# Grouped attention of a four-layer kernel: the out-projection with the weights held, 512 tokens moving, fp32r products on split parts, and sums turned back once per batch

## Chip, cores and metric

The kernel runs on 1 core of one Trainium2 chip. The metric is the device time of one execution in microseconds (us). Three runs of the kernel before gave 2711.46, 2713.54 and 2714.96 us, with a median of 2713.54 us.

## What is computed

Four layers run one after the other on 4 batches of 512 tokens with 256 features, all in float32. The first is a windowed attention with 16 heads of 128, the second is the block this change lies in, the third is another attention, and the fourth is a mixture of experts. Around each layer stand a layer norm and a residual sum. The second layer begins with a grouped attention, which is all that the change touches:

```python
# 32 query heads, 8 key and value heads, head size 64; x is (4, 512, 256)
h = _rms(x, ln_w)
q = (h @ wq).reshape(B, S, NHEADS, HEAD_DIM)
k = (h @ wk).reshape(B, S, KVHEADS, HEAD_DIM)
v = (h @ wv).reshape(B, S, KVHEADS, HEAD_DIM)
q, k = _rope(q, k)
...
scores = jnp.einsum('bqhd,bkhd->bhqk', q, k) / np.float32(np.sqrt(HEAD_DIM))
scores = jnp.where(causal[None, None], scores, jnp.float32(-1e+30))
attn = jax.nn.softmax(scores, -1)
o = jnp.einsum('bhqk,bkhd->bqhd', attn, v).reshape(B, S, NHEADS * HEAD_DIM)
x = x + o @ wo
```

The out-projection is `o @ wo`: 2048 inputs to 256 outputs for each token.

## The kernel before

`attention1` (L896) works in **units**. A unit M is one batch and two query heads (one head of each key/value head of a pair), so there are 16 units for a batch and 64 in all. A unit has four **steps** S = 4M + j, and step j works on the token tile `tile_of(S)`: 0, 2, 1, 3 for j = 0 to 3. Tile t has t+1 blocks of 128 keys, so the rows it handles are 128, 384, 256 and 512 wide in the order of the steps. Every engine has its own queue, in an order written out by hand in one loop over the steps, and the queues meet at semaphores.

- **TensorE** (L1079 to L1095): in step S the scores of both heads (L1033, into one of four front banks `b_f` each); in j = 1 of some units a projection for later work (`beside`, L908: the keys of the next pair in units with m % 4 = 1, the values of the next batch in four units of a batch); in j = 1 the first half of the out-projection of unit M-3 (L1070); the transposes of step S-3 (L1043, one back bank `b_t` for each head); in j = 0 the queries of unit M+2 (L1020) and then the values product of unit M-2 (L1057, a back bank too); in j = 3 the second half of the out-projection of unit M-3.
- There are **two back banks**, taken in turn by everything that writes `b_t`. `back_free` (L998) makes TensorE wait until what was in the bank two uses ago has been read.
- **ScalarE** (L1132 to L1141): in step S first the copies of the transposed blocks of step S-3 out of the two back banks (`copy_pt`, L1105), then the exponentials of step S (L1114), then in j = 0 the copy of the values product to `ot` (`copy_out`, L1121), and in j = 1 the copy of a projected tile of values (`copy_v`, L1128).
- **VectorE** (L1186 to L1198): mask and row minimum of step S straight from the front banks (L1166), the reciprocals of step S-1 (L1174), the rotary products of each query and key projection (L1152, L1155), and once a batch the addition of the finished out-projection to the residual (`add_y`, L1180).
- **GpSimd** (L1226 to L1233): the normalising product of step S-1 (L1221) and the sums that end the rotary embedding (L1214).

The out-projection of a unit before has the tokens held and the weights moving. Each of four token tiles is a product of 128 inputs x 128 tokens with 128 x 256 weights:

```python
for t in (2 * half, 2 * half + 1):
    x = pe.matmul(p_y[half][:, t % 2 * DIM:(t % 2 + 1) * DIM], ot[:, M % 3, t * P:(t + 1) * P], wo[:, m, :],
                  start=(m == 0 and t % 2 == 0), stop=(m == B_UNITS - 1 and t % 2 == 1),
                  skip_group_check=True)
```

The banks `p_y` hold tokens in rows and sum over the 16 units of a batch. A float32 product stands in the trace as two matmul records (a transpose as one). Below, "the transposes of tile 3" are those of the step whose rows are 512 wide, 4 for each of two heads, and "the transposes of tile 0" are the two of the step with 128. In the first layer (`attention0`, not touched) the projections at L207 are already made in the manner that the change brings here: three fp32r products on a high and a low part of each operand; L342 and L565 there write such a high and such a low part.

Of the kernel before, what the change touches and what calls it, by code (L numbers as in the profile page):

```python
# [895 lines left out]
def attention1(nc, c, tables_in, wo_in):  # L896
# [19 lines left out]

    HEAD = [("v", 0, t) for t in range(TB)] + [("k", 0, 0), ("q", 0, 0), ("q", 1, 0)]
    fronts, backs = list(HEAD), []
    for S in range(LAST):
# [9 lines left out]
        if j == 0 and 0 <= M - 2 < UNITS:  # L929
            backs.append(("o", M - 2, 0))  # L930
    FRONT = {use: at for at, use in enumerate(fronts)}
# [4 lines left out]
    with ExitStack() as st:  # L936
# [15 lines left out]
        ot = sb("ot", [P, 3, SEQ])  # L952
# [7 lines left out]
        s_ov, s_ot, s_y, s_xn = sem("pv"), sem("ot_copied"), sem("out_proj"), sem("added")  # L960

# [15 lines left out]
        with nc.Block() as block:  # L977
# [7 lines left out]
            def _(pe):  # L985
# [12 lines left out]
                def back_free(use):  # L998
# [4 lines left out]
                    if kind == "t":  # L1003
                        pe.wait_ge(s_pt, 2 * i + n + 1)
                    else:
                        pe.wait_ge(s_ot, i + 1)
# [54 lines left out]
                def out_proj(M, half):  # L1061
                    m, b = M % B_UNITS, M // B_UNITS
                    if half == 0:
                        pe.wait_ge(s_ot, M + 1)
                        if m == 0 and b > 0:
                            pe.wait_ge(s_xn, b)
                        if M == 0:
                            pe.wait_ge(s_wo, 16)
                    for t in (2 * half, 2 * half + 1):
                        x = pe.matmul(p_y[half][:, t % 2 * DIM:(t % 2 + 1) * DIM], ot[:, M % 3, t * P:(t + 1) * P], wo[:, m, :],  # L1070
                                      start=(m == 0 and t % 2 == 0), stop=(m == B_UNITS - 1 and t % 2 == 1),
                                      skip_group_check=True)
                    if half == 1:
                        x.then_inc(s_y, 1)

# [3 lines left out]
                for S in range(LAST):  # L1079
# [12 lines left out]
                    if j == 0 and 0 <= M - 2 < UNITS:  # L1092
                        values(M - 2)
                    if j == 3 and ends:
                        out_proj(M - 3, 1)  # L1095

            @block.scalar
            def _(act):
# [18 lines left out]
                def copy_out(M):  # L1117
                    act.wait_ge(s_ov, M + 1)
                    if M >= 3:
                        act.wait_ge(s_y, M - 2)  # L1120
                    act.activation(ot[:, M % 3, :], back_bank(("o", M, 0))[:, :], ACT.Copy).then_inc(s_ot, 1)  # L1121
# [10 lines left out]
                for S in range(LAST):  # L1132
# [11 lines left out]
            def _(dve):  # L1144
# [1560 lines left out]
```

## Time and profile before

| | before |
|---|---|
| median of 3 runs | 2713.54 us |
| the profiled execution | 2709.55 us |
| its span | 2707.4 us |
| TensorE busy | 2346.0 us, 87% of the span |
| VectorE busy | 1624.5 us, 60% |
| ScalarE busy | 1299.8 us, 48% |
| GpSimd busy | 1294.4 us, 48% |
| TensorE records at L1070 (the out-projection changed here) | 512, 134.9 us busy |

The span is the time from the first to the last instruction of one profiled execution; that execution took 2709.55 us. Shares are means over four layers with different limits, so the stage of the change has to be read by itself. The grouped attention lasts from about 672 to 1502 us of the span. A record's own duration is longer than the time it keeps the engine from the next one, since matmuls and activations overlap with what follows; what an instruction costs its queue is the distance from its start to the next start.

### The profile page before, as it was taken

The numbers are of one execution on the slowest core, as the hardware profiler recorded it, in microseconds if no ns is written. First come the engines' busy times: TensorE is split into PE (matmuls) and PEld (weight loads), VectorE is DVE, ScalarE is ACT, GpSimd is POOL, SyncE is SP. The second block draws the span as 40 slices with busy tenths as digits, with TensorE's granted clock in tenths as the row PEclk, the third lists the DMA queues.
The fourth block names the chain that finished last, engine by engine and source line by source line (L and its number), as shares of the span: only waits on it lengthen the run. The fifth ranks groups of instructions, "written<-read, shape, count | busy, mean of one in ns | idle before, by whom it ended". The sixth has DMA issues, their size and how long they took to land. (4 is left out here: it accounts for less than half of the span.)

```text
span 2707.4 us, 41000 instructions
## 1 busy us (share of the span) xinstructions
PE 2346.0 (87%) x12100; PEld 1565.0 (58%) x12100; DVE 1624.5 (60%) x5263; ACT 1299.8 (48%) x3690; POOL 1294.4 (48%) x1301
## 2 busy tenths in 40 slices
PE   5999999996899999999999599992688887699992
PEld 5888888895455555555555456551334343566661
DVE  5767767666766766766776543335766753553334
ACT  3444444444555656656666344432265565343332
POOL 2444545441555555555555158870534310038883
PEclk8999999998999999999999689995799998699996
DMA  5000000011000000000000635553000000515555
GB/s 172 1 16 15 15 15 15 15 52 43 1 1 1 1 1 1 1 1 1 2 1 1 255 63 87 85 80 90 0 0 1 1 1 1 203 36 86 87 85 121
DMA packets 72817, 112.25 MB, mean 41 GB/s; under 512 B 11504, under 2 KB 59632, under 8 KB 72240
## 3 DMA queue, kind: packets, MB, share of 16 engines
q0 software_dynamic: 30336, 42.73, 10.1%
q1 hardware_dynamic: 42304, 67.34, 7.2%
q8 instruction: 88, 1.44, 0.2%
q14 instruction: 89, 0.73, 0.1%
HBM read 80.69 MB, written 36.32 MB: 43 GB/s over the span
## 5 line engine op out<-in xcount | busy, mean ns | idle before, releaser
L1221 POOL TENSOR_TENSOR b_sm<-b_sm,b_rden 128x128 f32<-128x128 f32 (+3 forms) x512 | 355.0, 720 | 355.5 <-DVE b_rden L1174 355.4
L1114 ACT ACTIVATE b_sm<-b_sm,b_mn 128x128 f32<-128x128 f32 (+3 forms) x512 | 284.8, 568 | 22.9 <-DVE b_mn L1166 21.6
L1105 ACT ACTIVATE b_pt<-b_t 128x128 f32<-128x128 f32 (+3 forms) x512 | 195.2, 438 | 143.1 <-PE b_t L1043 143.0
L1166 DVE CUSTOM_DVE_ANT_0 b_sm<-b_f,maskB 128x128 f32<-128x128 f32 (+3 forms) x512 | 233.5, 489 | 2.8 <-issue 1.7
L1033 PE MATMUL b_f<-b_k,b_q 64*128 64x128 f32 (+3 forms) x1024 | 209.6, 485 | 28.9 <-DVE b_prod L1155 14.5
L1155 DVE SCALAR_TENSOR_TENSOR b_prod<-b_f,b_sin 32x512 f32<-32x512 f32 x320 | 219.8, 687 | 4.3
L1590 POOL DMA_INDIRECT XN<-rows,m_slots x158 | 157.7, 998 | 94.0 <-issue 47.5
L2195 ACT ACTIVATE c_pt<-c_second 128x512 f32<-128x512 f32 x256 | 139.2, 598 | 123.6 <-PE c_second L2061 123.3
L2310 DVE TENSOR_REDUCE c_nm<-c_first 128x2 f32<-128x1024 f32 x128 | 155.1, 1220 | 69.8 <-PE c_first L2048 69.8
L1043 PE MATMUL b_t<-ident,b_sm 128*128 128x128 f32 x1280 | 193.2, 281 | 1.1 <-ACT b_pt L1105 0.8
L1043 PEld LDWEIGHTS b_t<-ident,b_sm 128*128 128x128 f32 x1280 | 142.2, 141 | 87.5 <-issue 60.3
L537 POOL TENSOR_TENSOR a_q<-a_prod 128x512 f32<-128x512 f32 x64 | 81.6, 1275 | 230.4 <-DVE a_prod L425 230.4
L1409 PE MATMUL m_p<-WM,Y 128*128 x316 | 153.8, 610 | 1.3 <-issue 1.3
L1057 PE MATMUL b_t<-b_pt,Y 128*64 128x512 f32 (+3 forms) x1024 | 152.0, 439 | 2.5 <-ACT b_pt L1105 2.5
L1020 PE MATMUL b_f<-HT,b_w 128*128 128x512 f32 x320 | 153.7, 604 | 0.0
L358 ACT ACTIVATE a_s<-a_s,a_nmx 128x192 f32<-128x192 f32 (+1 forms) x256 | 110.0, 431 | 89.0 <-DVE a_nmx L438 89.0
L1597 POOL DMA_INDIRECT acc<-Y,m_slots x79 | 125.3, 1587 | 32.6 <-issue 20.2
L1597 POOL DMA_INDIRECT acc<-m_plain,m_slots x79 | 125.4, 1587 | 30.1 <-issue 20.7
L1057 PEld LDWEIGHTS b_t<-b_pt,Y 128*64 128x64 f32 x1024 | 68.4, 136 | 117.1 <-issue 78.8
L1070 PE MATMUL b_y<-b_wo,b_ot 128*128 128x256 f32 x512 | 134.9, 387 | 0.0
L1033 PEld LDWEIGHTS b_f<-b_k,b_q 64*128 64x128 f32 x1024 | 78.7, 186 | 86.8 <-issue 62.2
L1787 DVE COPY Y<-m_p 128x256 f32<-128x256 f32 x79 | 33.5, 425 | 153.1 <-PE m_p L1419 133.7
(325 smaller groups left out, 5341.7 us busy)
## 6 DMA issues: line engine op xcount, KB each, us to landing
WM<-in_m_w_dram SPq DMA_DIRECT2D x4, 3072.0 KB, 17.2
WM<-in_m_w_dram SPq DMA_DIRECT2D x4, 2432.0 KB, 14.6
acc<-in_zeros_dram SPq DMA_DIRECT2D x3, 2176.0 KB, 15.2
n_part<-acc SPq DMA_DIRECT2D x12, 512.0 KB, 7.7
a_wa<-in_a_wa_dram SPq DMA_DIRECT2D x8, 512.0 KB, 4.3
b_w<-in_b_w_dram SPq DMA_DIRECT2D x1, 3072.0 KB, 10.3
XN<-rows,m_slots POOLq DMA_INDIRECT x158
X<-in_x_dram SPq DMA_DIRECT2D x4, 512.0 KB, 5.7
```

The source lines that it names most:

```text
L1033: pe.matmul(front_bank(("s", S, head))[:, 0:keys(t)], q_r[r, M % 3, t * P:(t + 1) * P], k_r[r, pg % 2, 0:keys(t)], start=True, stop=True). ...
L1043: x = pe.transpose(bank[:, k * P:(k + 1) * P], sm[:, slot(S, head), k * P:(k + 1) * P], c.ident[:, :])
L1057: x = pe.matmul(bank[r:r + B_HD, k * P:SEQ], v_s[:, b % 2, k, pair * P + r:pair * P + r + B_HD], pt[:, M % 2, head, k, k * P:SEQ], start=( ...
L1105: act.activation(pt[:, M % 2, head, 0:t + 1, t * P:(t + 1) * P], back_bank(("t", S, head))[:, 0:keys(t)].rearrange("p (k n) -> p k n", n=P ...
L1114: act.activation(sm[:, s, 0:keys(t)], sm[:, s, 0:keys(t)], ACT.Exp, scale=-1.0, bias=mn[:, s:s + 1], accum_out=den[:, s:s + 1]).then_inc(s ...
L1155: x = dve.scalar_tensor_tensor(to[dst, 1, :], bank[src, :], scale, sin[src, :], ALU.mult, ALU.mult)
L1166: dve.tensor_tensor_reduce(sm[:, s, 0:keys(t)], front_bank(("s", S, head))[:, 0:keys(t)], mask[:, SEQ - keys(t):SEQ], 1.0, -3 * NEG, ALU.a ...
L1221: pool.tensor_tensor(sm[:, s, 0:keys(t)], sm[:, s, 0:keys(t)], rden[:, s:s + 1].to_broadcast([P, keys(t)]), ALU.mult).then_inc(s_pn, 1)
L1409: x = pe.matmul(p_h[j % 2][:, 0:HC], lhs, rhs, start=(k == 0), stop=(k == 1))
L1590: pool.indirect_dma_start(out=xg[:, b % RING, :], out_offset=None, in_=rows_dram[:, :], in_offset=IOA(ap=slots[:, b:b + 1], axis=0)).then_ ...
L1597: pool.indirect_dma_start(out=acc_dram[b % 2][:, :], out_offset=IOA(ap=slots[:, b:b + 1], axis=0), in_=ys[:, b % 4, :], in_offset=None, co ...
L2310: dve.tensor_reduce(nm[:, t, 2 * j:2 * j + 2], two_banks(("max", f)), AX.X, ALU.max, negate=True).then_inc(s_nm, 1)
```

## The change

The out-projection of a unit holds the weights and lets the 512 tokens of the batch move: for each half of the 256 outputs three fp32r products (high weights by high sums, high by low, low by high). The banks `p_y` then hold outputs in rows and tokens in columns. For this `ot` and the unit's weights are each split: ScalarE copies the high parts (`ot_hi`, `wo_hi`, both fp32r) and GpSimd subtracts to get the low ones (`ot_lo`, `wo_lo`). Once per batch VectorE copies the two banks to `y_t`, TensorE transposes them back in two halves of four transposes, each into a back bank, and VectorE adds each to the residual.

```diff
+    def turned_back(S):
+        M, j = S // STEPS_OF, S % STEPS_OF
+        if j == 2 and M >= B_UNITS and M % B_UNITS in (4, 5):
+            return ("z", M // B_UNITS - 1, M % B_UNITS - 4)
+        return None
...
+        if turned_back(S) is not None:
+            backs.append(turned_back(S))
+    backs += [("z", BATCH - 1, half) for half in range(2)]
...
                     if kind == "t":
                         pe.wait_ge(s_pt, 2 * i + n + 1)
+                    elif kind == "z":
+                        pe.wait_ge(s_xn, 2 * i + n + 1)
...
                 def out_proj(M, half):
                     m, b = M % B_UNITS, M // B_UNITS
                     if half == 0:
-                        pe.wait_ge(s_ot, M + 1)
+                        pe.wait_ge(s_ol, M + 1)
                         if m == 0 and b > 0:
-                            pe.wait_ge(s_xn, b)
-                        if M == 0:
-                            pe.wait_ge(s_wo, 16)
-                    for t in (2 * half, 2 * half + 1):
-                        x = pe.matmul(p_y[half][:, t % 2 * DIM:(t % 2 + 1) * DIM], ot[:, M % 3, t * P:(t + 1) * P], wo[:, m, :],
-                                      start=(m == 0 and t % 2 == 0), stop=(m == B_UNITS - 1 and t % 2 == 1),
+                            pe.wait_ge(s_yc, b)
+                        pe.wait_ge(s_wl, M + 1)
+                    cols = slice(half * P, (half + 1) * P)
+                    w_hi, w_lo = wo_hi[:, M % 3, cols], wo_lo[:, M % 3, cols]
+                    o_hi, o_lo = ot_hi[:, M % 2, :], ot_lo[:, M % 2, :]
+                    for n, (weight, o) in enumerate(((w_hi, o_hi), (w_hi, o_lo), (w_lo, o_hi))):
+                        x = pe.matmul(p_y[half][:, :], weight, o, start=(m == 0 and n == 0), stop=(m == B_UNITS - 1 and n == 2),
                                       skip_group_check=True)
...
+                def turn_back(use):
+                    _, b, half = use
+                    pe.wait_ge(s_yc, b + 1)
+                    back_free(use)
+                    for t in range(2):
+                        for k in range(KD):
+                            at = (2 * half + t) * P
+                            x = pe.transpose(back_bank(use)[:, t * DIM + k * P:t * DIM + (k + 1) * P], y_t[:, k, at:at + P],
+                                             c.ident[:, :])
+                    x.then_inc(s_z, 1)
...
+                    if turned_back(S) is not None:
+                        turn_back(turned_back(S))
                     if j == 3 and ends:
                         out_proj(M - 3, 1)
+                for half in range(2):
+                    turn_back(("z", BATCH - 1, half))
...
+                def high_out(M):
+                    act.wait_ge(s_ot, M + 1)
+                    if M >= 2:
+                        act.wait_ge(s_y, M - 1)
+                    act.activation(ot_hi[:, M % 2, :], ot[:, M % 2, :], ACT.Copy).then_inc(s_oh, 1)
+
+                def high_weights(M):
...
+                    act.activation(wo_hi[:, M % 3, :], wo[:, M % B_UNITS, :], ACT.Copy).then_inc(s_wh, 1)
...
+                    if j == 1 and 0 <= M - 2 < UNITS:
+                        high_out(M - 2)
+                        high_weights(M - 2)
...
-                def add_y(b):
+                def copy_y(b):
                     dve.wait_ge(s_y, (b + 1) * B_UNITS)
-                    for a in range(2):
-                        to = c.XN[:, b * TB + 2 * a:b * TB + 2 * a + 2, :].rearrange("p t d -> p (t d)")
-                        x = dve.tensor_tensor(to, p_y[a][:, :], to, ALU.add)
-                    x.then_inc(s_xn, 1)
+                    if b > 0:
+                        dve.wait_ge(s_z, 2 * b)
+                    for k in range(2):
+                        x = dve.tensor_copy(y_t[:, k, :], p_y[k][:, :])
+                    x.then_inc(s_yc, 1)
+
+                def add_y(use):
+                    _, b, half = use
+                    dve.wait_ge(s_z, 2 * b + half + 1)
+                    to = c.XN[:, b * TB + 2 * half:b * TB + 2 * half + 2, :].rearrange("p t d -> p (t d)")
+                    dve.tensor_tensor(to, back_bank(use)[:, :], to, ALU.add).then_inc(s_xn, 1)
...
+                    if S >= 1 and turned_back(S - 1) is not None:
+                        add_y(turned_back(S - 1))
...
+                def low_weights(M):
+                    pool.wait_ge(s_wh, M + 1)
...
+                    pool.tensor_tensor(wo_lo[:, M % 3, :], wo[:, M % B_UNITS, :], wo_hi[:, M % 3, :].bitcast(F32),
+                                       ALU.subtract).then_inc(s_wl, 1)
+
+                def low_out(M):
+                    pool.wait_ge(s_oh, M + 1)
...
+                    pool.tensor_tensor(ot_lo[:, M % 2, :], ot[:, M % 2, :], ot_hi[:, M % 2, :].bitcast(F32),
+                                       ALU.subtract).then_inc(s_ol, 1)
...
+                    if j == 3 and 0 <= M - 2 < UNITS:
+                        low_weights(M - 2)
+                        low_out(M - 2)
+                for M in range(UNITS - 2, UNITS):
+                    low_weights(M)
+                    low_out(M)
```

`copy_out` now also waits for the low part of the unit before the last, and `ot` has two buffers where it had three.

How the queues change is shown at three places. The first is ScalarE's queue over one unit, from the copies of tile 1 (128x2x128) to the copy to `ot`. Before:

```order
L1105 ACTIVATE b_pt<-b_t 128x2x128 x2
L1114 ACTIVATE b_sm,b_den<-b_sm,b_mn 128x384 x2
L1105 ACTIVATE b_pt<-b_t 128x4x128 x2
L1114 ACTIVATE b_sm,b_den<-b_sm,b_mn 128x256 x2
L1105 ACTIVATE b_pt<-b_t 128x128 x2
```

And with the change (L1137 are the copies of L1105, L1146 the exponentials of L1114):

```order
L1137 ACTIVATE b_pt<-b_t 128x2x128 x2
L1146 ACTIVATE b_sm,b_den<-b_sm,b_mn 128x384 x2
L1159 ACTIVATE b_ot_hi<-b_ot 128x512
L1166 ACTIVATE b_wo_hi<-b_wo 128x256
L1137 ACTIVATE b_pt<-b_t 128x4x128 x2
L1146 ACTIVATE b_sm,b_den<-b_sm,b_mn 128x256 x2
L1137 ACTIVATE b_pt<-b_t 128x128 x2
```

Two copies stand between the exponentials and the copies of tile 3, and so ahead of the copies that free the back banks for tile 0.

The second place is TensorE's queue in the unit after the one in which VectorE copied the sums of a batch, with the transposes that turn them back (L1100; L1059 are the transposes of L1043, L1049 the scores, L1088 the out-projection):

```order
L1088 MATMUL b_y<-b_ot_hi,b_wo_lo 128x512
L1059 MATMUL b_t<-ident,b_sm 128x128 x4
L1049 MATMUL b_f<-b_k,b_q 128x256 x2
L1059 MATMUL b_t<-ident,b_sm 128x128 x8
L1100 MATMUL b_t<-ident,b_y_t 128x128 x4
L1049 MATMUL b_f<-b_k,b_q 128x512 x2
L1059 MATMUL b_t<-ident,b_sm 128x128 x2
```

Before, the same stretch of TensorE's queue read:

```order
L1043 MATMUL b_t<-ident,b_sm 128x128 x4
L1033 MATMUL b_f<-b_k,b_q 128x256 x2
L1043 MATMUL b_t<-ident,b_sm 128x128 x8
L1033 MATMUL b_f<-b_k,b_q 128x512 x2
L1043 MATMUL b_t<-ident,b_sm 128x128 x2
```

Four transposes with a bank of their own stand between those of tile 3 and those of tile 0. The third place is VectorE's queue at the same point (L1214 is the mask and minimum, L1222 the reciprocals, L1236 the addition to the residual):

```order
L1213 MEMSET tick 128x1
L1214 ISA b_sm,b_mn<-b_f,maskB 128x512
L1214 ISA b_mn 128x1
L1222 RECIPROCAL b_rden<-b_den 128x1 x2
L1236 TENSOR_TENSOR XN<-b_t,XN 128x512
L1213 MEMSET tick 128x1
L1214 ISA b_sm,b_mn<-b_f,maskB 128x128
```

The addition that empties that bank comes after the minima and reciprocals of the step that TensorE issues after the turning back.

## Rows read from the trace of the kernel before

**Rows 1.** Busy time by stretch: PE, PEld, DVE, ACT, POOL, then PEclk, DMA share, GB/s

```profile
1000.00:1400.00 400.00, 390.39 (x2082) 214.56 (x2082) 284.26 (x1212) 246.31 (x796) 222.09 (x291) 1.00 0.00 1
```

**Rows 2.** Waits between 1000 and 1400 us: total us, times, longest

```profile
ACT b_pt L1105 <- PE b_t L1043: 71.1, 31, 3.2
DVE tick L1165 <- PE b_f L1033: 58.1, 86, 2.3
```

**Rows 3.** Timeline of TensorE, a plain unit: start us, us, engine, line, operation

```profile
1134.80 1.13 PE L1070 MATMUL b_y<-b_wo,b_ot 128*128 128x256 f32 x4
1135.77 0.60 PE L1043 MATMUL b_t<-ident,b_sm 128*128 128x128 f32 x4
...
1136.93 1.09 PE L1043 MATMUL b_t<-ident,b_sm 128*128 128x128 f32 x8
1137.95 1.13 PE L1033 MATMUL b_f<-b_k,b_q 64*128 64x512 f32 x4
1139.01 0.44 PE L1043 MATMUL b_t<-ident,b_sm 128*128 128x128 f32 x2
1139.29 1.03 PE L1070 MATMUL b_y<-b_wo,b_ot 128*128 128x256 f32 x4
1140.24 0.49 PE L1033 MATMUL b_f<-b_k,b_q 64*128 64x128 f32 x4
...
1146.34 1.13 PE L1070 MATMUL b_y<-b_wo,b_ot 128*128 128x256 f32 x4
```

**Rows 4.** Timeline of ScalarE in the same unit

```profile
1136.18 0.66 ACT L1105 ACTIVATE b_pt<-b_t 128x256 f32<-128x256 f32 x2 [1.52 <-PE b_t L1043]
1136.73 0.62 ACT L1114 ACTIVATE b_sm<-b_sm,b_mn 128x384 f32<-128x384 f32 x1
...
1137.92 1.08 ACT L1105 ACTIVATE b_pt<-b_t 128x512 f32<-128x512 f32 x2
1138.88 0.52 ACT L1114 ACTIVATE b_sm<-b_sm,b_mn 128x256 f32<-128x256 f32 x1
```

**Rows 5.** Groups of instructions in the first layer: busy us, mean ns

```profile
L565 POOL TENSOR_TENSOR a_wb_parts<-a_wb,a_wb_parts 128x512 fp32r<-128x512 f32 x8 | 10.2, 1271 | 52.3 <-ACT a_wb_parts L342 52.3
...
L342 ACT ACTIVATE a_wb_parts<-a_wb 128x512 fp32r<-128x512 f32 x8 | 4.9, 617 | 0.0
```

**Rows 6.** Timeline of TensorE in the first layer, fp32r products with 512 moving

```profile
403.77 1.55 PE L207 MATMUL p_q<-HT_part,a_wa_parts 128*128 128x512 f32 x6
405.16 1.53 PE L207 MATMUL p_k<-HT_part,a_wa_parts 128*128 128x512 f32 x6
406.52 3.62 PE L274 MATMUL p_s<-a_wo,a_ot 128*128 128x256 f32 x16
```

**Rows 7.** Timeline of a unit with a key projection beside it

```profile
959.12 1.13 PE L1033 MATMUL b_f<-b_k,b_q 64*128 64x512 f32 x4 [0.72 <-DVE b_prod L1155]
960.17 0.44 PE L1043 MATMUL b_t<-ident,b_sm 128*128 128x128 f32 x2
...
958.30 1.07 ACT L1105 ACTIVATE b_pt<-b_t 128x512 f32<-128x512 f32 x2
```

**Rows 8.** Timeline of a unit with a values projection beside it

```profile
972.35 0.59 ACT L1128 ACTIVATE Y<-b_f 128x512 f32<-128x512 f32 x1
...
972.83 1.08 ACT L1105 ACTIVATE b_pt<-b_t 128x512 f32<-128x512 f32 x2
973.08 1.13 PE L1033 MATMUL b_f<-b_k,b_q 64*128 64x512 f32 x4 [0.64 <-ACT Y L1128]
```

**Rows 9.** Timeline of VectorE in the plain unit of rows 3

```profile
1139.25 0.69 DVE L1166 CUSTOM_DVE_ANT_0 b_sm<-b_f,maskB 128x512 f32<-128x512 f32 x1
...
1140.49 0.22 DVE L1174 RECIPROCAL b_rden<-b_den 128x1 f32<-128x1 f32 x2
```

**Rows 10.** Timeline of GpSimd in the same unit

```profile
1140.73 3.18 POOL L1221 TENSOR_TENSOR b_sm<-b_sm,b_rden 128x256 f32<-128x256 f32 x4 [0.58 <-DVE b_rden L1174]
```

**Rows 11.** Timeline of the stage's end

```profile
1496.67 3.72 PE L1070 MATMUL b_y<-b_wo,b_ot 128*128 128x256 f32 x16
...
1496.79 0.60 ACT L1121 ACTIVATE b_ot<-b_t 128x512 f32<-128x512 f32 x1 [2.53 <-PE b_t L1057]
...
1500.43 1.29 DVE L1180 TENSOR_TENSOR XN<-b_y,XN 128x512 f32<-128x512 f32 x2 [12.47 <-PE b_y L1070]
```

More of the change, by code:

```diff
@@ L951, in attention1 @@
         pt = sb("pt", [P, 2, 2, TB, SEQ])
-        ot = sb("ot", [P, 3, SEQ])
+        ot, ot_hi, ot_lo = sb("ot", [P, 2, SEQ]), sb("ot_hi", [P, 2, SEQ], F32R), sb("ot_lo", [P, 2, SEQ], F32R)
+        wo_hi, wo_lo = sb("wo_hi", [P, 3, DIM], F32R), sb("wo_lo", [P, 3, DIM], F32R)
+        y_t = sb("y_t", [P, 2, SEQ])
         front, back = [pb(f"f{i}") for i in range(4)], [pb(f"t{i}") for i in range(2)]
@@ L960, in attention1 @@
         s_ov, s_ot, s_y, s_xn = sem("pv"), sem("ot_copied"), sem("out_proj"), sem("added")
+        s_oh, s_ol, s_wh, s_wl = sem("ot_high"), sem("ot_low"), sem("wo_high"), sem("wo_low")
+        s_yc, s_z = sem("y_copied"), sem("y_turned_back")
         def tile_of(S):
@@ L1118, in copy_out @@
                     act.wait_ge(s_ov, M + 1)
+                    if M >= 2:
+                        act.wait_ge(s_ol, M - 1)
+                    act.activation(ot[:, M % 2, :], back_bank(("o", M, 0))[:, :], ACT.Copy).then_inc(s_ot, 1)
+                def high_out(M):
+                    act.wait_ge(s_ot, M + 1)
+                    if M >= 2:
+                        act.wait_ge(s_y, M - 1)
+                    act.activation(ot_hi[:, M % 2, :], ot[:, M % 2, :], ACT.Copy).then_inc(s_oh, 1)
+                def high_weights(M):
+                    if M == 0:
+                        act.wait_ge(s_wo, 16)
                     if M >= 3:
                         act.wait_ge(s_y, M - 2)
-                    act.activation(ot[:, M % 3, :], back_bank(("o", M, 0))[:, :], ACT.Copy).then_inc(s_ot, 1)
+                    act.activation(wo_hi[:, M % 3, :], wo[:, M % B_UNITS, :], ACT.Copy).then_inc(s_wh, 1)
                 def copy_v(job):
@@ L1192, in _ @@
                     if j == 0 and M > 3 and M % B_UNITS == 3:
-                        add_y(M // B_UNITS - 1)
+                        copy_y(M // B_UNITS - 1)
+                    if S >= 1 and turned_back(S - 1) is not None:
+                        add_y(turned_back(S - 1))
                     if j == 0 and M + 2 < UNITS:
@@ L1197, in _ @@
                         rotate(beside(M))
-                add_y(BATCH - 1)
+                copy_y(BATCH - 1)
+                for half in range(2):
+                    add_y(("z", BATCH - 1, half))
             @block.gpsimd
@@ L1222, in normalise @@
                                            ALU.mult).then_inc(s_pn, 1)
+                def low_weights(M):
+                    pool.wait_ge(s_wh, M + 1)
+                    if M >= 3:
+                        pool.wait_ge(s_y, M - 2)
+                    pool.tensor_tensor(wo_lo[:, M % 3, :], wo[:, M % B_UNITS, :], wo_hi[:, M % 3, :].bitcast(F32),
+                                       ALU.subtract).then_inc(s_wl, 1)
+                def low_out(M):
+                    pool.wait_ge(s_oh, M + 1)
+                    if M >= 2:
+                        pool.wait_ge(s_y, M - 1)
+                    pool.tensor_tensor(ot_lo[:, M % 2, :], ot[:, M % 2, :], ot_hi[:, M % 2, :].bitcast(F32),
+                                       ALU.subtract).then_inc(s_ol, 1)
                 for job in HEAD[TB:]:
```

## The prediction

> **What bounds the kernel now.** I read the busy time by stretch first. In the middle of the grouped attention TensorE is busy 390 of 400 us at its full granted clock (1.00, the 2.4 GHz level); VectorE is at 284, ScalarE at 246, GpSimd at 222 [rows 1]. That says TensorE's work sets the stage. The waits agree: ScalarE waits for transposes and VectorE for scores [rows 2]. A saving on TensorE would then count in full, and work added to ScalarE or GpSimd would be free. The mean hides who is *just* in time, so the timelines of one unit come next. A plain unit runs from 1134.80 to 1146.34 us, 11.54 us [rows 3]. ScalarE idles before the copies of tile 1, then runs without a gap: copies of tile 1 at 1136.18, exponentials of 384 at 1136.73, copies of tile 3 from 1137.92 to 1139.00 [rows 4]. TensorE needs the back bank of the second of these for the second transpose of tile 0. The two transposes start at 1139.01 and the next product at 1139.29 [rows 3], so one takes about 0.13 us and the second starts at 1139.14. A bank or buffer that ScalarE frees reaches TensorE about 0.11 to 0.14 us after its copy's end (972.35 + 0.59 = 972.94, scores at 973.08 [rows 8]); I take 0.11. So the second transpose could not have begun before 1139.11. **This link has 0.03 us to spare**, and that is exactly where the change puts two copies.
>
> **The change part by part.**
>
> *Out-projection on TensorE.* Before, a half costs 1135.77 − 1134.80 = 0.97 and 1140.24 − 1139.29 = 0.95 us [rows 3]. Sixteen such records in a row at the end take about 3.72 − 0.38 = 3.34 us to the last start, 0.22 each [rows 11], so 4 are 0.86 to 0.89 and some 0.1 is the first weight load after narrower work. An fp32r product with 512 moving costs (405.16 − 403.77)/6 = 0.232 and (406.52 − 405.16)/6 = 0.227 us [rows 6]; three are 0.69, with the same first load 0.80. So **0.16 to 0.17 us less for a half, 0.34 for a unit**. Without the first load it would be 0.5 for a unit. That is small because a float32 product of 256 already costs only about twice an fp32r product of 512.
>
> The Trainium skill (TensorE: Matmul & The Clock Gate, Back-to-back issue gap) gives about 131 ns as the sustained spacing at 512 moving columns. By that the saving would be about 0.9 us a unit; the rows here say 0.23 us for the same count, in a stream with weight loads, and the sum goes by them.
>
> *Two copies on ScalarE, each unit.* Copies of 512 cost (1138.88 − 1137.92)/2 = 0.48 us start to start, of 256 (1136.73 − 1136.18)/2 = 0.275 [rows 4]. A copy from SBUF to fp32r lasts 617 ns [rows 5] where `copy_out` from PSUM lasts 0.60 [rows 11]; so 0.02 more. Together **0.78 us**. They lie between the exponentials of 384 and the copies of tile 3. These then end at 1139.00 + 0.78 = 1139.78, and TensorE's second transpose starts at 1139.89 instead of 1139.14: a stall of 0.75 us. The half saved ahead of it moves both queues alike. A plain unit comes to 0.75 − 0.34 = +0.41 us. Behind the stalled transpose stand the other half of the out-projection, the scores of the next unit and the queries' projection, so nothing passes it. Bounds of the two copies: 0.62 (a fifth off) and 617 + 400 ns of whole duration, 1.0.
>
> The Trainium skill (ScalarE: Activation LUTs, Rules for kernel authors) budgets about 0.3 us for each ACTIVATE plus 0.83 ns an element: 0.73 + 0.51 = 1.24 us for the pair, an estimate from that page. It would put about 20 us on the sum. The trace shows the next copy starting 0.48 us after one of 512, so I stay with the rows.
>
> *Units with a values projection.* Here TensorE already waits 0.64 us for `copy_v` [rows 8], which stands behind the new copies in ScalarE's queue: +0.78 − 0.34 = +0.44 us.
>
> *Units with a key projection.* Here the scores of 512 wait 0.72 us for VectorE's rotary products, and the copies of tile 3 end at 959.37, so the transpose at 960.17 + 0.13 has 0.8 us to spare [rows 7]. The new copies fit. The first half's saving is lost in VectorE's wait, the second's stays: −0.17 us.
>
> *GpSimd.* Low weights and low sums are subtractions of 256 and 512 columns; 512 cost 1271 ns [rows 5]; half the columns cost at least half, I take 0.73; 2.0 us in all. They follow the normalising of tile 1, which starts at 1140.73 and takes some 1.2 of the 3.18 us (two of the four products, the narrower ones) [rows 10]; with ScalarE's 0.78 of delay that ends at 1142.7, the low parts at 1144.7. The out-projection needs them at 1146.3, and GpSimd has 178 of 400 us idle [rows 1]. Cost zero while those 1.6 us hold; if they went, every excess would stall the first half directly.
>
> *Turning back.* Twice per batch, for three batches inside the loop. In a plain unit, the turned back half needs the bank of tile 3's first head, copied at 1137.92 + 0.78 + 0.60 = 1139.30; TensorE starts at 1139.41 instead of going on at 1137.95. Four transposes take 0.51 us (8 take 1.02 [rows 3]), so the scores of 512 start at 1139.92. VectorE starts its minimum 1.30 us after the scores, which started at 1137.95, and ends its reciprocals at 1140.71, 1.46 later [rows 9]; then comes the addition of about 0.65 to 0.69 (two in 1.29 [rows 11]). The bank is free at 1139.92 + 1.30 + 1.46 + 0.69 + 0.11 = 1143.48, and the second transpose of tile 0 waits for it: 4.34 us later than 1139.14, and no second stall for ScalarE. Net +4.0 us. The other half falls in a unit with a key projection; the same sum from 958.30 gives a start at 963.69 instead of 960.30, net +3.2 us. The two copies of VectorE take the place and about the time of the two old additions.
>
> *End.* Before: values, copy to `ot` until 1497.39, last product, additions from 1500.43 to 1501.72 [rows 11]. TensorE had the out-projection of the unit before last as cover. Now the last unit's copy is followed by the high copies (about 1.0 with the hand-over), the low weights (0.73) and low sums (1.27), then six products (1.4), their drain, two copies (1.3), eight transposes with an addition behind each half (about 2): the end falls near 1505.7, **+4 us**.
>
> *Sum.* The copies run for units 2 to 63: 14 with a key and 12 with a values projection, 3 plain and 3 key units with a turned back half, 33 other plain ones. 33 × 0.41 + 12 × 0.44 − 11 × 0.17 + 3 × 4.0 + 3 × 3.2 + 4 = 13.5 + 5.3 − 1.9 + 12 + 9.6 + 4 = **+42.5 us**. Against the profiled execution's 2709.55 us that is 2752 us. The median of the runs shown lies 4 us above that execution, 2756 from there; I say 2753. A measurement of this kernel can tell 0.2%, about 5 us, from no change.
>
> **The rivals.**
> A. *TensorE alone sets the stage* (ends faster). Place: the banks at tile 0's transposes. If ScalarE's two copies cost its queue less than about 0.34 us a unit, or TensorE has unseen slack there, no stall comes and the turned back halves cost only their 0.51 us: −62 × 0.34 + 3 + 4 = −14 us, 2696. For: 97% busy, and ScalarE 38% idle [rows 1]. Against: 0.03 us of slack by the rows, and no copy of 256 or 512 that costs so little. 7%.
> B. *The copies hide, the turned back halves don't*: −21 + 18 + 4, about 2711, no change. 6%.
> C. *The products come at the faster spacing.* If an fp32r product of 512 cost 0.13 us, as one of 256 might, each half would save 0.3 more: 48 units with two halves that count and 14 with one are −33 us, 2720. The skill's spacing named above would do this. Against: rows 6. 5%.
> D. *Dearer copies.* At 1.0 to 1.24 us a pair the 45 units that stall add 10 to 20 us: 2763 to 2773. The ScalarE page's rule is this one. 10%.
> E. *GpSimd is late.* If the subtractions cost over 3.6 us a unit (1.6 more than the rows), or are held back behind VectorE, the first half waits; a further 0.5 us on each of 62 units gives 2784. 4%.
> That the products split into more passes (the change not doing what it says) would need fp32r at 512 to act otherwise than in rows 6; it lies in what is left with E.
>
> **How the numbers follow.** The forecast has 66%, its own range 2740 to 2762 from the bounds of the copies (45 units × 0.16 to 0.22) and a turned back half a quarter cheaper. With A 7, B 6, C 5, D 10, E 4 and 2 for the rest, the range 2718 to 2774 leaves out A, B and E. Faster: A, some of B: 9%. Within 0.2%: most of B: 5%. Slower: 86%.
>
> **What the changed profile would show.** Right: the grouped attention lasts about 873 us instead of 830; TensorE's share in its middle falls toward 91%; waits of TensorE for the copies of tile 3 of about 0.75 us in plain units, which were absent; the scores after a values projection wait 1.4 us; six waits of about 2 us for the addition to the residual; an out-projection half of about 0.8 us; no waits for GpSimd's low parts. Wrong: plain units of 11.2 us with no wait at tile 0 (A); waits on the subtractions (E); three products in about 0.4 us (C).

## The result, and the profile after

Four runs of the changed kernel gave 2760.72 to 2773.98 us with a median of **2766.59 us**; the kernel before gave 2714.05 us (median of 4). The ratio is 1.0199, with a 95% interval of 1.0184 to 1.0215: slower, by 52.5 us, where 2753 was forecast in a range of 2718 to 2774. The number lies inside that range, but above the forecast's own 2740 to 2762.

| | before | after |
|---|---|---|
| median | 2714.05 us | 2766.59 us |
| profiled execution (span) | 2709.55 (2707.4) us | 2773.98 (2772.2) us |
| first scores of the stage to its last residual addition | 683.5 to 1501.7: 818.2 us | 682.9 to 1554.3: 871.4 us |
| plain unit | 11.54 us | 12.03 us |
| unit with a key projection | 14.05 us | 13.87 us |

The profiled execution after was the slowest of its four, and 11.6 us of its longer span lie outside the stage: most of them in the third layer, not touched, where it was granted a lower clock in places (0.93 against 0.98 in the stretch of its middle). So the stage's own length, **+53.2 us**, is what the readings below go by, and it is close to the difference of the medians (52.5).

The busy time by stretch, in the columns of [rows 1]:

```profile
1000.00:1400.00 400.00, 365.57 (x1900) 193.72 (x1900) 266.48 (x1140) 256.55 (x812) 267.93 (x335) 0.99 0.00 1
```

TensorE fell from 390 to 366 us busy in 400. It has not handed the bound to an engine that is full: the next, GpSimd, stands at 268. TensorE now waits. The whole execution's waits of TensorE for its own operands, in the order of the trace's answer on the lines of the scores and of the transposes:

```profile
  ACT Y L1173: 17.5, 12
  DVE b_prod L1203: 16.0, 14
...
  ACT b_pt L1137: 20.3, 68
```

`b_pt` are the copies out of the back banks: 68 waits where there were 2. `Y` is the copy of projected values: 12 waits, each 1.46 us where it was 0.64. The same answer names GpSimd's normalising product (`b_sm`) for another 54.8 us ahead of these transposes (13.6 before); that GpSimd isn't what they wait for is shown below by e4 and e6. Now a plain unit on TensorE, the rows that answer to [rows 3]:

```profile
1142.58 0.50 PE L1088 MATMUL b_y<-b_ot_hi,b_wo_hi 128*128 128x512 f32 x1
1142.92 0.39 PE L1088 MATMUL b_y<-b_ot_lo,b_wo_hi 128*128 128x512 f32 x1
1143.15 0.39 PE L1088 MATMUL b_y<-b_ot_hi,b_wo_lo 128*128 128x512 f32 x1
1143.38 0.60 PE L1059 MATMUL b_t<-ident,b_sm 128*128 128x128 f32 x4
...
1145.56 1.13 PE L1049 MATMUL b_f<-b_k,b_q 64*128 64x512 f32 x4
1147.10 0.30 PE L1059 MATMUL b_t<-ident,b_sm 128*128 128x128 f32 x1 [0.40 <-ACT b_pt L1137]
1147.58 0.30 PE L1059 MATMUL b_t<-ident,b_sm 128*128 128x128 f32 x1 [0.19 <-ACT b_pt L1137]
1147.64 0.48 PE L1088 MATMUL b_y<-b_ot_hi,b_wo_hi 128*128 128x512 f32 x1
...
1148.51 0.49 PE L1049 MATMUL b_f<-b_k,b_q 64*128 64x128 f32 x4
```

And ScalarE's queue at the same time, against [rows 4]:

```profile
1145.54 0.62 ACT L1159 ACTIVATE b_ot_hi<-b_ot 128x512 fp32r<-128x512 f32 x1
1146.06 0.41 ACT L1166 ACTIVATE b_wo_hi<-b_wo 128x256 fp32r<-128x256 f32 x1
1146.36 1.07 ACT L1137 ACTIVATE b_pt<-b_t 128x512 f32<-128x512 f32 x2
```

The first half of the out-projection takes 1143.38 − 1142.58 = 0.80 us. The two copies take 1146.36 − 1145.54 = 0.82 us of ScalarE's queue. The copies of tile 3 end at 1147.43, and the second transpose of tile 0 starts at 1147.58, 0.15 us behind them, instead of the 1146.75 that TensorE's own queue ahead of it (1145.56 + 1.06 + 0.13) would allow: a stall of 0.83 us. The half behind it starts 0.06 us after that transpose (0.15 before) and takes 1148.51 − 1147.64 = 0.87 us (0.95 before): 0.17 us saved from the transpose on, as much as in the first half.

A unit with a turned back half, against the working in the prediction:

```profile
953.05 0.63 PE L1100 MATMUL b_t<-ident,b_y_t 128*128 128x128 f32 x4 [1.46 <-ACT b_pt L1137]
...
956.28 0.68 DVE L1236 TENSOR_TENSOR XN<-b_t,XN 128x512 f32<-128x512 f32 x1
...
957.10 0.30 PE L1059 MATMUL b_t<-ident,b_sm 128*128 128x128 f32 x1 [2.10 <-POOL b_sm L1280]
957.16 0.51 PE L1088 MATMUL b_y<-b_ot_hi,b_wo_hi 128*128 128x512 f32 x1
957.48 0.62 PE L1088 MATMUL b_y<-b_ot_lo,b_wo_hi 128*128 128x512 f32 x1
957.89 0.63 PE L1088 MATMUL b_y<-b_ot_hi,b_wo_lo 128*128 128x512 f32 x1
```

The first wait is the 1.46 us that the prediction's rows give (1137.95 to 1139.41). The second is named after GpSimd's normalising, but that transpose waits for two things, and the other one came last: VectorE's addition that empties the bank (`add_y`), which starts at 956.28 and takes 0.68 us, so it ends 0.14 us before the transpose. In e1 below, three of the six waits of 2.10 us are named after this addition. A releaser's name in such a row is a hint, the queue's own order decides. The unit took 15.59 us from second transpose to second transpose (941.51 to 957.10), the one with the key projection after it 18.84 (to 975.94).

The records after 957.4 show something else: 0.62 us where such a product is 0.39. The granted clock of the stretches behind the wait:

```profile
941.00:957.00 16.00, 12.33 (x67) 6.63 (x67) 9.99 (x45) 10.08 (x33) 10.12 (x15) 1.00 0.00 1
957.00:962.00 5.00, 4.90 (x18) 3.25 (x18) 0.70 (x8) 3.41 (x11) 4.39 (x5) 0.66 0.02 3
962.00:967.00 5.00, 5.00 (x25) 2.04 (x24) 4.24 (x10) 0.62 (x2) 0.14 (x1) 1.00 0.00 0
```

For some of the 5 us after the two waits TensorE ran at the lower level (1.2 GHz). The Trainium skill (TensorE: Matmul & The Clock Gate, HAM oscillation) says that waits between stretches of TensorE's work can bring its clock down. The trace agrees in part: with the same waits of 1.46 and 2.10 us ahead, the clock fell behind the first turned back half of each of the three batches (0.66, 0.72 and 0.76 over the next 5 to 7 us) and stayed at the full level behind the second half of each (1.00 over the next 5 us).

The same happens at two other places, and it matters for the comparisons below. In the second unit of the stage TensorE waits 1.18 and 2.29 us in every kernel here. The kernel before goes on at the full clock, the changed one doesn't, and its unit takes 1.27 us more. The stretch from 708 to 712 us, before and after:

```profile
708.00:712.00 4.00, 3.80 (x18) 1.77 (x16) 2.33 (x20) 3.87 (x15) 3.82 (x5) 1.00 0.01 2
708.00:712.00 4.00, 4.00 (x13) 2.39 (x14) 1.90 (x15) 3.41 (x13) 4.00 (x6) 0.57 0.01 2
```

In this unit e3 and e4 of the experiments below ran at the lower level too, and e1, e2 and e5 to e9 at the full one. The other place is the last unit's six products, behind a wait of 2.09 us: 0.43 us apart in the kernel after, 0.23 in e1, e2 and e3. Each of the two is worth 1.2 to 1.9 us of stage. No edit explains them: e1 and e3 run the same instructions in the second unit, and e3 and e7 in the last products, and still differ there.

### The profile page after: what moved, and what is told of

Same layout as the page of the kernel before. It is cut to its first block and busy times, and to the rows that moved or that the text cites. A ratio compares the mean times of both kernels' runs of the same rounds, so it can differ in the third digit from the quotient of the medians.

```text
span 2772.2 us, 41329 instructions
## 1 busy us (share of the span) xinstructions
PE 2356.4 (85%) x12004; PEld 1555.1 (56%) x12004; DVE 1632.3 (59%) x5271; ACT 1350.7 (49%) x3818; POOL 1418.1 (51%) x1429
## 5 line engine op out<-in xcount | busy, mean ns | idle before, releaser
L1146 ACT ACTIVATE b_sm<-b_sm,b_mn 128x128 f32<-128x128 f32 (+3 forms) x512 | 284.9, 569 | 19.0 <-DVE b_mn L1214 18.9
L1137 ACT ACTIVATE b_pt<-b_t 128x128 f32<-128x128 f32 (+3 forms) x512 | 196.2, 438 | 151.6 <-PE b_t L1059 151.0
L1049 PE MATMUL b_f<-b_k,b_q 64*128 64x128 f32 (+3 forms) x1024 | 210.0, 487 | 38.5 <-ACT Y L1173 17.5
L1214 DVE CUSTOM_DVE_ANT_0 b_sm<-b_f,maskB 128x128 f32<-128x128 f32 (+3 forms) x512 | 233.7, 489 | 3.7 <-issue 2.5
L1059 PE MATMUL b_t<-ident,b_sm 128*128 128x128 f32 x1280 | 201.9, 284 | 33.2 <-ACT b_pt L1137 20.3
L1059 PEld LDWEIGHTS b_t<-ident,b_sm 128*128 128x128 f32 x1280 | 145.4, 142 | 129.5 <-issue 71.7
L1049 PEld LDWEIGHTS b_f<-b_k,b_q 64*128 64x128 f32 x1024 | 79.1, 187 | 98.4 <-issue 79.1
L1213 DVE MEMSET tick<- 128x1 f32 x512 | 30.2, 59 | 160.1 <-PE b_f L1049 154.0
```

Source lines behind the costliest of these rows:

```text
L1049: pe.matmul(front_bank(("s", S, head))[:, 0:keys(t)], q_r[r, M % 3, t * P:(t + 1) * P], k_r[r, pg % 2, 0:keys(t)], start=True, stop=True). ...
L1059: x = pe.transpose(bank[:, k * P:(k + 1) * P], sm[:, slot(S, head), k * P:(k + 1) * P], c.ident[:, :])
L1137: act.activation(pt[:, M % 2, head, 0:t + 1, t * P:(t + 1) * P], back_bank(("t", S, head))[:, 0:keys(t)].rearrange("p (k n) -> p k n", n=P ...
L1146: act.activation(sm[:, s, 0:keys(t)], sm[:, s, 0:keys(t)], ACT.Exp, scale=-1.0, bias=mn[:, s:s + 1], accum_out=den[:, s:s + 1]).then_inc(s ...
L1214: dve.tensor_tensor_reduce(sm[:, s, 0:keys(t)], front_bank(("s", S, head))[:, 0:keys(t)], mask[:, SEQ - keys(t):SEQ], 1.0, -3 * NEG, ALU.a ...
```

## The experiments

The runs e1 to e4, e5 to e8 and e9 each have the kernel before measured beside them on the same chip. Stage lengths are from the first scores to the last residual addition, one profiled execution each; the kernel before has 818.2 us. Units of a kind that no edit touches take the same time within 0.03 us in all of them, except where the clock fell at the two places named above; where a comparison crosses these, their share is given. So the stage settles terms that the whole kernel's time, which scatters by some us for reasons in other layers, can't.

| run | whole, median us | before in that group | ratio, 95% interval | stage us |
|---|---|---|---|---|
| e1_high_early | 2721.78 | 2710.85 | 1.0048 (1.0032 to 1.0065) | 830.5 |
| e2_turn_early | 2738.47 | 2710.85 | 1.0108 (1.0091 to 1.0126) | 846.9 |
| e3_both_moves | 2700.13 | 2710.85 | 0.9964 (0.9952 to 0.9975) | 809.1 |
| e4_before_copies | 2751.37 | 2710.85 | 1.0150 (1.0133 to 1.0167) | 859.1 |
| e5_float32_held | 2714.64 | 2709.78 | 1.0013 (1.0003 to 1.0022) | 823.2 |
| e6_low_twice | 2702.39 | 2709.78 | 0.9968 (0.9955 to 0.9981) | 811.1 |
| e7_values_first | 2698.73 | 2709.78 | 0.9950 (0.9933 to 0.9967) | 801.3 |
| e8_one_product | 2667.77 | 2709.78 | 0.9839 (0.9822 to 0.9855) | 777.0 |
| e9_end_shorter | 2694.69 | 2714.17 | 0.9931 (0.9917 to 0.9944) | 798.4 |

**The place of the copies in ScalarE's queue.** The changed kernel, with:

```diff
                         copy_out(M - 2)
-                    if j == 1 and 0 <= M - 2 < UNITS:
                         high_out(M - 2)
                         high_weights(M - 2)
```

> ScalarE's two high copies are issued in step j = 0 right behind the copy to ot, where ScalarE has been idle, and no longer between the exponentials of 384 and the copies of tile 3. Theory (the copies' place in ScalarE's queue stalls TensorE at the transposes of tile 0): the waits there go, a plain unit takes about 11.25 us instead of 12.03, the wait behind a values projection falls from 1.46 to about 0.68 us, the waits before the turned back halves too; 51 times 0.78 = 40 us less than the changed kernel, about 2727 us. Rival (the split work loads GpSimd or memory, wherever it stands): no change, about 2766 us.

```profile
1137.15 1.13 PE L1049 MATMUL b_f<-b_k,b_q 64*128 64x512 f32 x4
1138.21 0.44 PE L1059 MATMUL b_t<-ident,b_sm 128*128 128x128 f32 x2
```

The stage fell from 871.4 to 830.5, by 40.9 us; 2.5 of them are the clock, which fell in the second unit and in the last products after, and did not here. The waits of TensorE for `b_pt` at tile 0 are down from 68 to the 2 that were there before the change, those behind a values projection are back at 0.64, and the wait before a turned back half is 0.64 where it was 1.46; the 2.10 us behind it stayed. A plain unit takes 11.21 us. The same two copies, the same subtractions and products, some 38 us apart by their place alone.

The reverse, the kernel before with only the copies added, in the place that the change gives them:

```diff
+                def high_copies(M):
+                    act.wait_ge(s_ot, M + 1)
+                    act.activation(ot_hi[:, M % 2, :], ot[:, M % 3, :], ACT.Copy)
...
+                    act.activation(wo_hi[:, M % 3, :], wo[:, M % B_UNITS, :], ACT.Copy)
...
+                    if j == 1 and 0 <= M - 2 < UNITS:
+                        high_copies(M - 2)
```

> The kernel before, with nothing but the two high copies added to ScalarE's queue where the change has them (nobody reads what they write). Theory: 36 plain units stall 0.75 us and 12 with a values projection 0.78 us, units with a key projection not at all: 36 us more than the kernel before, about 2750 us. Rival (TensorE alone sets the stage, ScalarE has 38% idle): no change, 2714 us.

The stage went to 859.1 us, +40.9, of which 1.2 are the clock in the second unit, and the whole kernel to 1.0150 of its time. The rows of two units:

```profile
1148.06 0.30 PE L1044 MATMUL b_t<-ident,b_sm 128*128 128x128 f32 x1 [0.40 <-POOL b_sm L1231]
1148.54 0.30 PE L1044 MATMUL b_t<-ident,b_sm 128*128 128x128 f32 x1 [0.19 <-ACT b_pt L1106]
1160.42 0.30 PE L1044 MATMUL b_t<-ident,b_sm 128*128 128x128 f32 x1 [0.40 <-POOL b_sm L1231]
```

A plain unit takes 12.36 us (1148.06 to 1160.42) where it took 11.54: 0.82, the whole of the copies' time, and so does a unit with a values projection; 48 × 0.82 = 39.4 us. Nothing was added to GpSimd here, and the first transpose still bears its name: the product that it reads (128x128) had ended at 1145.93, and ScalarE's first copy of tile 3 ended at 1147.93, 0.13 us ahead of it. Copies that nobody reads cost some 40 us on an engine that idles a third of the stage.

**The place of the turned back halves.** The changed kernel, with:

```diff
-        if j == 2 and M >= B_UNITS and M % B_UNITS in (4, 5):
+        if j == 0 and M >= B_UNITS and M % B_UNITS in (4, 5):
...
-                    if S >= 1 and turned_back(S - 1) is not None:
-                        add_y(turned_back(S - 1))
                     if j == 0 and M + 2 < UNITS:
                         rotate(("q", M + 2, 0))
+                    if turned_back(S) is not None:
+                        add_y(turned_back(S))
```

> Only the turned back halves move: TensorE issues them in step j = 0 behind the values product, VectorE adds them behind the rotary products of the same step. Theory (a half costs because of the banks that it waits for and holds, not for its four transposes): a unit with a turned back half falls from 15.6 to about 12.6 us (plain) and from 18.8 to about 14.5 us (key); 22 us less than the changed kernel, about 2744 us, and TensorE's granted clock stays at 1.00 in these units. Rival (the transposes and additions themselves are the price): at most 3 us less.

```profile
940.42 0.30 PE L1059 MATMUL b_t<-ident,b_sm 128*128 128x128 f32 x1 [0.40 <-ACT b_pt L1137]
...
947.09 0.66 PE L1100 MATMUL b_t<-ident,b_y_t 128*128 128x128 f32 x4
947.67 0.92 PE L1049 MATMUL b_f<-b_k,b_q 64*128 64x384 f32 x4
...
953.03 0.30 PE L1059 MATMUL b_t<-ident,b_sm 128*128 128x128 f32 x1 [0.40 <-POOL b_sm L1280]
```

No wait before the four transposes, and 947.67 − 947.09 = 0.58 us for them. The unit takes 12.61 us where it took 15.6 and a plain one takes 12.03. The stage fell by 24.5 us, and the granted clock of 700 to 1000 and of 1000 to 1400 us is 1.00 where it was 0.99. So six halves had cost over 4 us each for 0.58 us of work. Of the 24.5, 22.1 lie in the units with the halves, as was expected; some 4.7 of them are the lower clock behind the waits (worked out below). The other 2.5 are the clock in the second unit and in the last products, where this edit changes nothing.

**Both moves**, the two diffs together:

> Both moves together. Theory: the saving of the products is left, 0.34 us for 48 units and 0.17 for 14, less 4 us for the turned back halves and 7 us for the longer end: about 8 us less than the kernel before, 2706 us. Rival (the new form of the out-projection does not pay at all): 2714 us or more. Rival (fp32r products at 0.13 us): under 2690 us.

The stage takes 809.1 us, 9.1 less than the kernel before (10.3 without the clock's 1.2 in the second unit), and the whole kernel is 0.36% faster than it. A plain unit takes 11.21 us:

```profile
980.07 1.13 PE L1049 MATMUL b_f<-b_k,b_q 64*128 64x512 f32 x4
981.13 0.44 PE L1059 MATMUL b_t<-ident,b_sm 128*128 128x128 f32 x2
981.32 0.48 PE L1088 MATMUL b_y<-b_ot_hi,b_wo_hi 128*128 128x512 f32 x1
...
982.19 0.49 PE L1049 MATMUL b_f<-b_k,b_q 64*128 64x128 f32 x4
```

That is 0.33 less than before, the saving of the products alone, with no wait at tile 0. The second half takes 0.87 us (981.32 to 982.19) without a stall ahead of it too. The change's arithmetic does pay; what it was charged for was order.

**Form or split.** The weights held and 512 tokens moving, but in float32, with the halves turned back early (no splitting at all):

```diff
-                    for n, (weight, o) in enumerate(((w_hi, o_hi), (w_hi, o_lo), (w_lo, o_hi))):
-                        x = pe.matmul(p_y[half][:, :], weight, o, start=(m == 0 and n == 0), stop=(m == B_UNITS - 1 and n == 2),
-                                      skip_group_check=True)
+                    x = pe.matmul(p_y[half][:, :], wo[:, m, cols], ot[:, M % 3, :], start=(m == 0), stop=(m == B_UNITS - 1),
+                                  skip_group_check=True)
```

> The weights held and 512 tokens moving, turned back early as in the second run, but as one float32 product for each half instead of three fp32r ones: no splitting on ScalarE and GpSimd. Theory (a float32 product of 512 costs 0.905 us as in the queries' projection, with the first weight load 1.0, against 0.96 for the half before): no saving on TensorE, 5 us more for the products, 4 for the turned back halves, 2 for the end; 2716 to 2722 us where the kernel before takes 2711. Rival (holding the weights with more columns moving is what pays): under 2705 us.

```profile
982.17 1.12 PE L1085 MATMUL b_y<-b_ot,b_wo 128*128 128x512 f32 x2
983.13 0.60 PE L1058 MATMUL b_t<-ident,b_sm 128*128 128x128 f32 x4
```

The halves take 0.96 and 0.95 us, where they took 0.97 and 0.95 with the tokens held [rows 3]; I had expected 1.0. Holding the weights gives float32 nothing, and the turning back, with the longer end that it brings (2.0), costs the 5 us by which the stage is longer. The saving is that of fp32r alone.

**GpSimd's load.** Both moves, with the subtraction for the low sums made twice:

```diff
+                                       ALU.subtract).then_inc(s_o2, 1)
+                    pool.wait_ge(s_o2, M + 1)
+                    pool.tensor_tensor(ot_lo[:, M % 2, :], ot[:, M % 2, :], ot_hi[:, M % 2, :].bitcast(F32),
```

> The kernel with both moves, with GpSimd's subtraction for the low sums done twice: 1.27 us more for it in each of 64 units. Theory (the low parts come over 1.6 us before they are used): at most 3 us more than without, 2700 to 2703 us, 1.3 of it at the end of the stage. Rival (GpSimd's load counts): 79 us more, 2779 us.

+2.0 us in the stage for 81 us more of work on GpSimd. Between the first unit and the last, leaving out the second unit, where here the clock did not fall (−1.2), it is +0.3 us. The end is 2.9 us longer: 1.3 in the wait for the low sums of the last unit (3.4 us instead of 2.1), and 1.3 because the products behind that wait ran at the lower clock. GpSimd's slack holds.

**A third place in ScalarE's queue.** Both moves, and the copy of projected values first in its step:

```diff
+                    if j == 1 and beside(M) is not None and beside(M)[0] == "v":
+                        copy_v(beside(M))
                     if 0 <= S - LAG < TOTAL:
                         copy_pt(S - LAG)
```

> The kernel with both moves, and ScalarE's copy of a projected tile of values ahead of the copies of tile 1 instead of behind the exponentials. Theory (the place in ScalarE's queue decides here too): the wait of 0.64 us in 12 units goes, 8 us less, about 2692 us. Rival: the copy delays the copies of tile 1 by as much as it gives, no change from 2700 us.

The stage fell by 7.8 us, to 801.3, and the twelve waits are gone: a unit with a values projection takes 12.93 us where it took 13.63, 8.5 us in twelve. (The clock gives 1.2 us in the second unit and takes 1.9 at the end.) This move doesn't need the change: `copy_v` stands in the kernel before too, with the same waits of 0.64 us [rows 8], and whether it would gain as much there wasn't run. The whole kernel's median fell by only 1.4 us, and the intervals of the two ratios overlap (0.9933 to 0.9967 against 0.9952 to 0.9975): of the whole the gain isn't shown, of the stage it is.

**What a product costs in place.** Both moves, with only the product of the high parts (the two products with low parts are left out):

> The kernel with both moves, but with the product of the high parts alone (the two products with low parts are left out; the splitting stays). Theory (0.23 us a product, TensorE sets the stage again once the copies have moved): 0.92 us less in 48 units, 0.46 in 14, 50 us less than 2700: 2650 us. Rival (another engine has become the bound at 11.2 us a unit): less than half of that, over 2675 us.

The stage fell by 32.1 us (1.2 of it the clock in the second unit), between the two: neither theory held. A unit with a values projection gained the full 0.92 us, one with a key projection 0.28, a plain one 0.46. TensorE's waits:

```profile
PE b_f L1049 <- DVE b_prod L1202: 23.3, 16, 2.3
PE b_f L1049 <- ACT Y L1173: 7.7, 12, 0.6
PE b_t L1059 <- ACT b_pt L1137: 7.5, 34, 0.8
```

With both moves alone the first is 17.3 us and the last 1.1, in 2 waits. A plain unit takes 10.75 us (first transposes of tile 0 at 1067.50 and 1078.26), the value of two products less and not of four. Its rows show where the other two went:

```profile
1067.70 0.48 PE L1088 MATMUL b_y<-b_ot_hi,b_wo_hi 128*128 128x512 f32 x1
1068.11 0.49 PE L1049 MATMUL b_f<-b_k,b_q 64*128 64x128 f32 x4
1068.78 1.10 PE L1059 MATMUL b_t<-ident,b_sm 128*128 128x128 f32 x6 [0.18 <-ACT b_pt L1137]
1069.72 1.88 PE L1036 MATMUL b_f<-HT,b_w 128*128 128x512 f32 x4
```

The second half takes 0.41 us instead of 0.87, but the scores behind it last 0.67 to the next transposes and these 0.94, where they last 0.42 and 0.71 with both moves alone: 0.48 us lost around six transposes that need the banks of tile 0, which ScalarE copies at 1068.36, behind a stretch without a gap. So below some 11 us a plain unit is set by ScalarE again, one link further on.

**The end of the stage.** The seventh run's kernel, with the last unit's six products in another order and GpSimd's low sums ahead of its low weights:

```diff
+                    for weight, o, ready in ((hi, o_hi, s_wh), (hi, o_lo, s_ol), (lo, o_hi, s_wl)):
+                        pe.wait_ge(ready, UNITS)
...
+                        for half in range(2):
+                            x = pe.matmul(p_y[half][:, :], weight[:, half * P:(half + 1) * P], o, start=False,
+                                          stop=(weight is lo), skip_group_check=True)
```

> The kernel with both moves and the values copied first, and for the last unit alone the six products in another order: both halves of high by high while GpSimd still subtracts, then both with the low sums, which GpSimd now makes before the low weights, then both with the low weights. Theory (at the end of the stage every one of these steps stands on the path): TensorE waits for the low parts in two pieces and only two products are left behind the last subtraction; about 1.7 us less than without, a stage of 799 to 800 us against 801.3; the whole about 2692 us, 18 us less than the kernel before. Rival (the granted clock falls in the wait and the products behind it take double): under 0.5 us.

```profile
1476.08 0.73 PE L1085 MATMUL b_y<-b_ot_hi,b_wo_hi 128*128 128x512 f32 x2
1477.03 0.73 POOL L1302 TENSOR_TENSOR b_wo_lo<-b_wo,b_wo_hi 128x256 fp32r<-128x256 f32 x1
1477.12 0.73 PE L1085 MATMUL b_y<-b_ot_lo,b_wo_hi 128*128 128x512 f32 x2 [0.31 <-POOL b_ot_lo L1309]
1477.82 0.73 PE L1085 MATMUL b_y<-b_ot_hi,b_wo_lo 128*128 128x512 f32 x2
1478.58 1.29 DVE L1244 COPY b_y_t<-b_y 128x512 f32<-128x512 f32 x2 [13.09 <-PE b_y L1085]
```

The stage is 798.4 us, 2.8 less than in e7. Not all of it is the order. In e7 the six products followed a wait of 2.09 us and came 0.43 us apart, at the lower clock level; in e3 they followed one of 2.10 us and came 0.23 apart. Against e3 the end is 1.2 us shorter, which is what the order gives; the rest is the clock that fell in e7. Whether a TensorE with something to do during the subtractions keeps its clock more often isn't shown by one execution of each. This kernel is **the fastest here that makes all the products: 2694.69 us, 0.9931 (0.9917 to 0.9944) of the kernel before**, the change's own idea with four things put elsewhere. Its interval overlaps that of e7 (0.9933 to 0.9967), so the last step is shown by the stage and not by the whole.

## Why the prediction was right, point by point

- **That ScalarE's two copies stall TensorE at tile 0's transposes** was the step on which it all hung, and it holds: shown by taking them away from there (−38 us without the clock's share) and by putting them alone into the kernel before (+40).
- **The size of the stall** is the term that was mis-sized in plain units: 0.83 us instead of 0.75. The copies cost 0.82 us, not 0.78: a 512 copy from SBUF to fp32r keeps the queue 0.52 us, not 0.50, and the one of 256 0.30, not 0.275. And the transpose starts 0.15 us behind the copies of tile 3, not 0.11, so the link had no slack where 0.03 was read from [rows 3] and [rows 4]. That is 0.08 × 33, 2.6 us.
- **The out-projection's saving** was put at 0.34 us a unit and is 0.34 (0.83 of stall less 0.49 of growth); in e3, without the stall, 0.33 is measured.
- **Values units**: the wait of 1.46 that the rows lead to is there (0.64 + 0.82), and the unit grew by 0.49 us (13.97 to 14.46) where 0.44 was forecast. **Key units**: 13.87 against 14.05, −0.18 as forecast, and TensorE's wait for VectorE rose from 0.72 to 0.89 us, which is the first half's saving being lost.
- **Turned back halves**: +4.05 us in the plain unit (forecast 4.0). In the key unit 4.79 where 3.2 was forecast. The prediction's own steps add up to 3.4 there (the transpose at 963.86 and not 963.69). It assumed the full clock throughout: from the start of the half at 957.16 to the values product at 962.52 it is 5.36 us, and 3.82 in a plain unit (1147.64 to 1151.46), so 1.54 us are the lower level. Three times that is some 4.7 us, the largest thing that the sum lacked. It was not on the list of rivals.
- **The end**: from the start of the last values product to the last addition 7.4 us before and 12.4 after, +5.0 where +4 was forecast. The last six products ran at the lower clock level, 1.3 us; without it the end is 3.7 longer.
- **The sum** with measured terms: 33 × 0.49 + 12 × 0.49 − 11 × 0.18 + 3 × 4.05 + 3 × 4.79 + 5.0 = 16.2 + 5.9 − 2.0 + 12.2 + 14.4 + 5.0 = 51.7 of the stage's 53.2 us. Of the last 1.5 us 1.3 are the clock in the second unit, which the sum had no term for.
- **The number**: +42.5 was forecast and +53.2 measured in the stage. Some 7 of the missing 10.7 us are the clock in these three kinds of place, the rest the stall's size. 2766.59 us lies where rival D (dearer copies, 2763 to 2773) would have put it, but not by D's mechanism. That the wider range held it is in part luck, since nothing in the prediction stood for the clock. TensorE's share in the middle of the stage is 91%, as said.
- **The rivals**: TensorE alone (A) and hidden copies (B) fall with e4. The faster spacing (C) falls with the rows: 0.23 us between products in every run at full clock, where the Trainium skill (TensorE: Matmul & The Clock Gate, Back-to-back issue gap) has some 131 ns as sustained spacing at 512; the measurement decides. The dearer copies (D) fall too: the trace gives 0.82 us for the pair. The rule of the Trainium skill (ScalarE: Activation LUTs, Rules for kernel authors) would make it 1.24, an estimate; it is stated for an ACTIVATE that reads its bias through a pointer, and the rows of these copies show no such operand. GpSimd (E) falls with e6.

## What to carry to other kernels

An engine with a third of its time idle can still stand on the path in one link of each round: before work is added to a queue, read from the timeline when the instruction behind it is needed, in hundredths of a us, and put the work where that queue has been idle. Whatever takes a turn in a rotation of two banks should empty its bank ahead of any work that the waiting engine has yet to feed; here that was worth 4 us each time for 0.58 us of transposes. And a change that measures slower may be a good one in the wrong order: the one here was 2% slower as written and 0.36% faster than the kernel before once its copies and its halves were moved. With the last products and the copy of projected values moved too it is 0.7%, but the last of these may well help the kernel before as much. When single executions are compared, compare the granted clock at the same places first: here it moved the stage by up to 2.5 us between kernels that do the same work there.

## What was not expected of the hardware

TensorE's clock fell after some waits and not after others of the same length. Behind 1.46 and 2.10 us of waiting in one unit of the changed kernel it fell in three of six cases; behind 1.18 and 2.29 us in the second unit in three of eleven executions; behind one of about 2.1 us ahead of the last six products in two (after, e7) of five. Where it fell it cost 1.2 to 1.9 us on top of the wait. What decides between the cases isn't shown. And a float32 product took the same 0.96 us for 128 x 128 weights under 512 moving columns as for two of 256: in these two forms the time goes by columns moved, whichever operand is held.
